# Cross attention, Mamba block and cross attention in one program: the same instructions in another order on five engines

## The chip, the core and the metric

The kernel runs on one core of a Trainium2 chip. The core has a matrix engine (PE), a vector engine (DVE), an activation engine (ACT), a general engine (POOL) and an engine that here only issues DMAs (SP). Each takes its own instructions strictly in order; between engines only semaphores order the work. The metric is the time of one execution on the device in microseconds (us), lower is better.

## What is computed

Input are 64 sequences of 128 tokens with 256 features (`x`) and as many of context (`ctx_1024`). Everything is computed for each sequence by itself, in float32.

```python
# layer 0: attention to the context, 16 heads of 16, masked queries, then layer norm
q, k, v = relu(x @ Wq + bq), relu(ctx @ Wk + bk), relu(ctx @ Wv + bv)
scores = where(mask_of_query, q k^T / sqrt(16), 1e-9)
x = layernorm(softmax(scores) @ v + x) * gamma + beta
# layer 1a: a Mamba block, 8 heads of 64, state of 128
zxbcdt = rms(x, norm_w) @ in_proj_w                       # z | xBC | dt
xBC = silu(conv_b + causal convolution of xBC over 4 taps)
dt = softplus(dt + dt_bias); decay = exp(dt * -exp(A_log))
h_t = h_(t-1) * decay_t + (dt_t * xh_t) outer B_t;  y_t = h_t C_t + D_skip * xh_t
x = x + rms(y * silu(z), gnorm_w) @ out_proj_w
# layer 1b: layer norm, then attention to the context, 8 heads of 32
x = x + softmax(LN(x) Wq (ctx Wk)^T / sqrt(32) + padding) @ (ctx Wv) @ Wo
```

## The kernel before

**Groups and halves.** Two sequences are a group; there are 32 groups (`NG`) of two halves (`NB`). All 32 go through one software pipeline that is written out by hand. A small function is a unit of work on one engine: `tap(g, 7)` is one of the 18 convolution steps of group g, `scan(g, 1)` the scan of its second half. It waits for its semaphores, issues one or a few instructions and raises a semaphore. Each engine has a list of unit calls, and a loop over `s` (called a round here) runs the list once a round: `q(s - 2, 0)` works on group s - 2, `wp(s - 7, 0)` on the group that began five rounds earlier. The offsets need only agree within an engine, since nothing but semaphores ties the engines together. In the steady part each engine does the work of one group in a round, from six neighbouring groups.

**Order and banks.** The list sets the order of an engine. The table `USES` gives for each use of a PSUM bank (`("k1", 0, 4), 1` is: unit k1, part 0, four rounds behind, in bank 1) the order of the uses, and `bank()` works out from it which semaphore tells that the user before in the bank is done; PE waits for it.

**Units that are spoken of here,** with their lines. PE: `q`, `k`, `cp`, `z` are groups of six matmuls of L301; `v` L333 and L336; `sA` L355 and `sT` L386 and L391 are the scores of layer 0; `tn` L366; `av` L411; `ot`, `nt`, `bx`, `ht`, `tC` are transposes at L397; `bd` L456 transposes the decays; `gm` L486; `y` L508; `o` L522 and L523; `q1`, `k1` L535; `v1` L573; `sC` L593 and L597 are the scores of layer 1b; `oC` L622; `wp` L635 is the last projection. DVE: `dk` L847 copies the decays out of PSUM to `decT`; `scan` L883 builds the matrix `L` of decay products from `DB`; `lg` L892 multiplies it; `tap` L859, `xc` L872 convolution; `rc` L739, `xo` L749, `bs` L758, `bg` L764, `xs` L770, `x2` L780 are the end of layer 0; `mA` L718 and `mC` L968 row maxima; `k2` L706; `r1`, `hh` L928, `hs` L935, `hg`, `hm` the second norm; `nm` L730 and L732; `yd` L911; `sz` L900. POOL: `xr` L1457 adds `xt`, the token-major x, to the attention's output in `xa`; `rs` L1464 and L1466; `qm` L1449; `dx` L1484; `xd` L1493; `ga` L1502; `s2_` L1508 and L1510; `nC` L1532. ACT: `split_x` L1127 among others.

**The way of the decays.** `dk` writes decT; SP writes it to HBM (`dec_out`, L266), waits until it has landed, and reads it back broadcast to 128 partitions, 512 KB for each half (`dec_in`, L274), into `DB`. The scan of the half waits for that. `y` on PE needs the scan, and `bd` of the next group stands behind `y` on PE.

**SP** has nine units a round, all in one queue. A unit that waits holds all behind it.

```python
def load_t(g):
    if ok(g):
        if g > 0:
            e.wait_ge(s_xr, 2 * g)
        e.dma_start(xt[:, :, :], a["xt"][g]).then_inc(d_xt, 16)
```

There is one buffer each for xT, cT, cU and xt, so that a load waits until the group before has been read.

Of the kernel before, what the change touches and what calls it, by code (L numbers as in the profile page):

```python
# [12 lines left out]
NG = 32  # L13
# [20 lines left out]
]  # L34
STEPS = NG + 7


def program(nc, a):
    with ExitStack() as ctx:
# [171 lines left out]
        def sync(e):  # L211
# [84 lines left out]
        def tensor(e):  # L296
# [345 lines left out]
            for s in range(STEPS):  # L642
                gm(s - 5, 0)
                z(s - 5, 1)
                ht(s - 6, 1)
                av(s - 4, 6)
                bx(s - 5, 1)
                y(s - 5, 0)
                q1(s - 6, 0)
                av(s - 4, 7)  # L650
                q1(s - 6, 1)
                gm(s - 5, 1)
                ot(s - 4, 1)
                sC(s - 6, 0)
                k1(s - 4, 0)
                v(s - 3, 0)
                o(s - 5, 0)
                sA(s - 3, 0)
                wp(s - 7, 0)
                k1(s - 4, 1)  # L660
                y(s - 5, 1)
                nt(s - 4, 0)
                sA(s - 3, 1)
                tC(s - 6, 0)
                q(s - 2, 0)
                tC(s - 6, 1)
                dp(s - 4, 0)
                cp(s - 4, 0)
                q(s - 2, 1)
                cp(s - 4, 1)  # L670
                tC(s - 6, 2)
                tn(s - 3, 0)
                o(s - 5, 1)
                cp(s - 4, 2)
                tC(s - 6, 3)
                cp(s - 4, 3)
                oC(s - 6, 0)
                oC(s - 6, 1)
                v1(s - 4, 0)
                k(s - 2, 0)  # L680
                sT(s - 3, 0)
                bd(s - 4, 0)
                k(s - 2, 1)
                cp(s - 4, 4)
                av(s - 3, 0)
                ht(s - 5, 0)
                cp(s - 4, 5)
                tn(s - 3, 1)
                av(s - 3, 1)
                av(s - 3, 2)  # L690
                av(s - 3, 3)
                sT(s - 3, 1)
                ot(s - 3, 0)
                z(s - 4, 0)
                bx(s - 4, 0)
                av(s - 3, 4)
                av(s - 3, 5)

        def vector(e):
# [325 lines left out]
            for s in range(STEPS):  # L1025
                tap(s - 4, 1)
                tap(s - 4, 2)
                dc(s - 4, 0)
                dc(s - 4, 1)
                tap(s - 4, 3)  # L1030
                dc(s - 4, 2)
                r1(s - 5, 1)
                hm(s - 5, 0)
                xc(s - 4, 0)
                tap(s - 4, 4)
                dc(s - 4, 3)
                hh(s - 5, 1)
                dc(s - 4, 4)
                dc(s - 4, 5)
                tap(s - 4, 5)  # L1040
                dc(s - 4, 6)
                dc(s - 4, 7)
                dc(s - 4, 8)
                dc(s - 4, 9)
                dc(s - 4, 10)
                xc(s - 4, 1)
                hs(s - 5, 1)
                dc(s - 4, 11)
# [10 lines left out]
                xc(s - 4, 2)
                tap(s - 4, 12)  # L1060
                hm(s - 5, 1)
                tap(s - 4, 13)
                xc(s - 4, 3)
                tap(s - 4, 14)
                tap(s - 4, 15)
                tap(s - 4, 16)
                tap(s - 4, 17)
                k2(s - 2, 1)
                xc(s - 4, 4)
                xc(s - 4, 5)  # L1070
                rc(s - 3, 0)
                xo(s - 3, 0)
                scan(s - 4, 0)
                bs(s - 3, 0)
                bg(s - 3, 0)
                lg(s - 4, 0)
                xs(s - 3, 0)
                sz(s - 4, 0)
                sz(s - 4, 1)
                yd(s - 4, 0)  # L1080
                x2(s - 3, 0)
                scan(s - 4, 1)
                lg(s - 4, 1)
                mC(s - 5, 0)
                rc(s - 3, 1)
                xo(s - 3, 1)
                mC(s - 5, 1)
                kk1(s - 3, 0)
                bs(s - 3, 1)
                bg(s - 3, 1)  # L1090
                mC(s - 5, 2)
                mC(s - 5, 3)
                r1(s - 4, 0)
                rC(s - 5, 0)
                xs(s - 3, 1)
                x2(s - 3, 1)
                mA(s - 2, 0)
                mA(s - 2, 1)
                hh(s - 4, 0)
                mA(s - 2, 2)  # L1100
                mA(s - 2, 3)
                rC(s - 5, 1)
                fin(s - 6, 0)
                kk1(s - 3, 1)
                nm(s - 2, 0)
                yd(s - 4, 1)
                rC(s - 5, 2)
                nl(s - 3, 0)
                nl(s - 3, 1)
                mA(s - 2, 4)  # L1110
                mA(s - 2, 5)
                mA(s - 2, 6)
                mA(s - 2, 7)
                hs(s - 4, 0)
                rC(s - 5, 3)
                d0(s - 3, 0)
                d0(s - 3, 1)
                tap(s - 3, 0)
                hg(s - 4, 0)

        def scalar(e):
# [244 lines left out]
            for s in range(STEPS):  # L1366
                eA(s - 4, 0)
                eA(s - 4, 1)
                eA(s - 4, 2)
                ac(s - 5, 4)  # L1370
                he(s - 6, 0)
                th(s - 5, 3)
                eA(s - 4, 3)
                nt_(s - 4, 1)
                ac(s - 5, 5)
                ke(s - 3, 1)
                oa(s - 4, 0)
                th(s - 5, 4)
                th(s - 5, 5)
                hx(s - 6, 1)  # L1380
                eA(s - 4, 4)
                eA(s - 4, 5)
                xhe(s - 5, 0)
                eA(s - 4, 6)
                zt(s - 5, 0)
                eA(s - 4, 7)
                zt(s - 5, 1)
                split_x(s - 2)
                he(s - 6, 1)
# [264 lines left out]
```

## Time and profile before

| | us |
|---|---|
| median of 3 runs | 1593.8 (1592.28 to 1598.35) |
| the profiled execution | 1593.56 |
| its span, first to last instruction | 1591.5 |
| PE busy | 1433.3 (90% of the span) |
| DVE busy | 1317.2 (83%) |
| ACT busy | 1030.6 (65%) |
| POOL busy | 881.3 (55%) |
| mean granted clock of PE | 0.977 of full speed |
| DMA | 86.99 MB, 55 GB/s on the mean |

An engine's busy time is the sum of its instructions with overlap taken out; a matmul's end is modelled. "issue" as a releaser means that the profile shows no event that the engine waited for. Busy shares alone don't tell what sets the time: the rows below do, by stretch, by wait, by the chain and by single instructions.

### The profile page before, as it was taken

How to read it: one execution, taken by the hardware profiler on the slowest of the kernel's cores; microseconds unless marked ns; L12 is line 12 of the kernel's file. 1: busy time of each engine (PE TensorE's matmuls, PEld its weight loads, DVE VectorE, ACT ScalarE, POOL GpSimd, SP SyncE). 2: the span in 40 equal slices, each digit the busy share in tenths (PEclk: the TensorE clock that was granted, in tenths of full speed). 3: DMA queues.
4: the chain of work that ended last, by engine and by line, in shares of the span. 5: the costliest groups of instructions: out<-in, count | busy, mean ns of one | idle time of the engine just before them, and what ended most of it. 6: DMA issues, size and time to landing. Idle time of an engine off the chain costs nothing.

```text
span 1591.5 us, 43440 instructions
## 1 busy us (share of the span) xinstructions
PE 1433.3 (90%) x15912; PEld 1185.8 (75%) x15912; DVE 1317.2 (83%) x3115; ACT 1030.6 (65%) x3044; POOL 881.3 (55%) x1125
## 2 busy tenths in 40 slices
PE   1889999999999999989988888999999999999976
PEld 1677787877777877777877777877778787778764
DVE  5688888888888888878888888889888888888882
ACT  1546767766667766666766666766666766676664
POOL 6354564565555556544556554556555566556553
PEclk9998999999999999999999999999999999999998
DMA  4111122112122101212201212201212211211110
GB/s 140 42 57 57 49 65 65 42 35 64 56 63 64 62 16 63 65 55 65 65 25 51 64 55 64 64 14 64 65 55 65 65 34 42 64 55 49 48 34 20
DMA packets 41136, 86.99 MB, mean 55 GB/s; under 512 B 5728, under 2 KB 10976, under 8 KB 40928
## 3 DMA queue, kind: packets, MB, share of 16 engines
q1 hardware_dynamic: 40928, 84.23, 17.4%
q8 instruction: 129, 2.11, 0.6%
q14 instruction: 79, 0.65, 0.1%
HBM read 75.53 MB, written 8.68 MB: 53 GB/s over the span
## 4 chain that ended last, share of the span: by engine, by line
PE 43%; DVE 18%; POOL 13%; DMA 13%; ACT 6%; issue 4%; SPq 3%; DVEq 0%; POOLq 0%; ACTq 0%
DMA DB<-dec_scratch 12%; PE bank L301 11%; DVE L L883 5%; PE bank L397 5%; POOL DX L1484 4%; ACT PC L1339 4%; PE bank L522 4%; PE bank L635 4%; PE bank L573 4%; DVE L L892 3%; POOL Y L1502 2%; PE bank L508 2%; PE bank L386 2%; PE bank L355 2%; PE bank L622 2%
## 5 line engine op out<-in xcount | busy, mean ns | idle before, releaser
L859 DVE SCALAR_TENSOR_TENSOR ACC<-bank,cw,ACC 128x250 f32<-128x250 f32 (+2 forms) x576 | 271.5, 472 | 20.5 <-ACT ACC L1266 9.8
L883 DVE TENSOR_TENSOR_SCAN L<-DB,id 128x1024 f32<-128x1024 f32 x64 | 184.0, 2876 | 62.7 <-DMA DB<-dec_scratch 62.7
L1339 ACT ACTIVATE PC<-bank,stc 128x128 f32<-128x128 f32 x512 | 180.7, 377 | 77.6 <-DVE stc L968 76.8
L301 PE MATMUL bank<-xnT,wnl 128*128 128x256 f32 x640 | 199.2, 311 | 1.9 <-ACT PTA L1178 0.5
L301 PE MATMUL bank<-xnT,wnh 128*128 128x256 f32 x640 | 179.3, 280 | 0.0
L301 PE MATMUL bank<-xnL,wnh 128*128 128x256 f32 x640 | 179.1, 280 | 0.0
L1484 POOL TENSOR_TENSOR DX<-XC,pc 128x512 f32<-128x512 f32 x64 | 126.2, 1972 | 73.7 <-DVE XC L872 73.7
L718 DVE TENSOR_REDUCE sta<-bank 128x4 f32<-128x512 f32 x256 | 160.9, 680 | 2.8 <-PE bank L355 2.8
L1178 ACT ACTIVATE PTA<-bank 128x512 f32<-128x512 f32 x256 | 141.7, 595 | 8.6 <-PE bank L391 8.6
L1532 POOL TENSOR_TENSOR PC<-PC,stc 128x512 f32<-128x512 f32 x128 | 133.3, 1042 | 10.3 <-DVE stc L975 10.3
L1502 POOL TENSOR_TENSOR Y<-Y,SZ 128x512 f32<-128x512 f32 x64 | 88.8, 1388 | 90.1 <-DVE Y L911 90.1
L522 PE MATMUL bank<-wout,Y 128*128 128x256 f32 x512 | 124.4, 387 | 6.2 <-POOL SQ L1510 6.2
L301 PEld LDWEIGHTS bank<-xnT,wnl 128*128 128x128 f32 x640 | 121.3, 189 | 10.9 <-DVE KT L706 8.5
L1266 ACT ACTIVATE ACC<-bank,cw 128x256 f32<-128x256 f32 x192 | 107.7, 561 | 32.0 <-PE bank L301 27.9
L1524 POOL TENSOR_SCALAR stb<-stb 128x1 f32<-128x1 f32 x64 | 14.0, 219 | 204.8 <-DVE stb L941 204.8
L508 PE MATMUL bank<-L,XH 128*64 128x128 f32 x1024 | 72.9, 286 | 58.8 <-issue 53.5
L301 PEld LDWEIGHTS bank<-xnL,wnh 128*128 128x128 f32 x640 | 121.3, 190 | 0.0
L301 PEld LDWEIGHTS bank<-xnT,wnh 128*128 128x128 f32 x640 | 120.6, 188 | 0.0
L508 PEld LDWEIGHTS bank<-L,XH 128*64 128x64 f32 x1024 | 57.7, 140 | 76.3 <-issue 73.9
L1283 ACT ACTIVATE XH<-bank 128x512 f32<-128x512 f32 x64 | 38.3, 598 | 114.3 <-PE bank L508 89.7
L1339 ACT ACTIVATION_READ_ACCUMULATOR PC<-bank,stc 128x1 f32 x512 | 110.8, 216 | 0.0
L522 PEld LDWEIGHTS bank<-wout,Y 128*128 128x128 f32 x512 | 93.8, 193 | 17.9 <-DVE L L892 3.9
(185 smaller groups left out, 4343.9 us busy)
## 6 DMA issues: line engine op xcount, KB each, us to landing
DB<-dec_scratch SPq DMA_DIRECT2D x64, 512.0 KB, 7.6
xT<-in_xT SPq DMA_DIRECT2D x32, 256.0 KB, 2.7
cT<-in_cT SPq DMA_DIRECT2D x32, 256.0 KB, 2.8
cU<-in_cT SPq DMA_DIRECT2D x32, 256.0 KB, 2.9
xt<-in_xt SPq DMA_DIRECT2D x32, 256.0 KB, 5.0
out_x<-X SPq DMA_DIRECT2D x32, 256.0 KB, 8.1
QM<-qm_rows SPq DMA_DIRECT2D x32, 128.0 KB, 3.1
XC<-in_win SPq DMA_DIRECT2D x2, 644.0 KB, 5.2
```

The source lines that it names most:

```text
L301: mm = e.matmul(t[:, c0:c0 + T], wt[:, k, m:m + 128], x[:, k, :], start=(n == 0), stop=(n == 5))
L508: mm = e.matmul(t[64 * (h % 2):64 * (h % 2) + 64, (h // 2) * 128:(h // 2 + 1) * 128], XH[:, h * 64:h * 64 + 64], L[:, h, :], start=True, s ...
L522: e.matmul(t[:, 0:256], Y[b][:, kk * 128:(kk + 1) * 128], wout[:, kk, :], start=(kk == 0), stop=(kk == 3))
L718: e.tensor_reduce(sta[ns % 4][:, 4 * j:4 * j + 4], t[:, :].rearrange("p (i k) -> p i k", i=4), AX_X, ALU.max, negate=True).then_inc(s_mA, 1)
L859: e.scalar_tensor_tensor(out=w, in0=t[:, 0:T].rearrange("p (b t) -> p b t", b=NB)[:, :, 0:125 + k], scalar=cw[:, c, k:k + 1], in1=w, op0=A ...
L883: e.tensor_tensor_scan(L[:, :, :].rearrange("p h t -> p (h t)"), DB[b][:, :], id8[:, :, :].rearrange("p h t -> p (h t)"), 0.0, ALU.mult, A ...
L1178: e.activation(PTA[n % 4][:, :, :], t[:, :].rearrange("p (i k) -> p i k", i=4), ACT.Exp).then_inc(s_eA, 1)
L1266: e.activation(ACC[n % 3][:, :, :], t[:, 0:T].rearrange("p (b t) -> p b t", b=NB), ACT.Identity, bias=cw[:, c, 4:5], scale=cw[:, c, 3:4]). ...
L1339: op = e.activation(PC[n % 5][:, p, :], t[:, p * 128:(p + 1) * 128], ACT.Exp, bias=stc[g % 4][:, 4 * i + p:4 * i + p + 1], accum_out=stc[g ...
L1484: e.tensor_tensor(cv(DX[:, :]), XC[g % 2][:, 0:4, b * 128:(b + 1) * 128], pc[:, 14:18].unsqueeze(2).to_broadcast([128, 4, 128]), ALU.mult) ...
L1502: e.tensor_tensor(cv(Y[b][:, :]), cv(Y[b][:, :]), SZ[:, :, b * 128:(b + 1) * 128], ALU.mult).then_inc(s_ga, 1)
L1532: e.tensor_tensor(PC[n % 5][:, :, :], PC[n % 5][:, :, :], stc[g % 4][:, 16 + 4 * i:20 + 4 * i].unsqueeze(2).to_broadcast([128, 4, 128]), A ...
```

## The change

No instruction is added, taken away or altered. The lists of all five engines are permuted, with them the table USES (other banks, other order), and the offsets of the units in their rounds. STEPS goes from NG + 7 to NG + 11 since SP's offsets are larger by a constant. The DVE, ACT, PE and POOL lists have 100, 66, 55 and 26 unit calls as before. The diff, cut to SP and to the places that matter here:

```diff
 USES = [
-    (("gm", 0, 5), 5), (("z", 1, 5), 3), (("ht", 1, 6), 6), (("bx", 1, 5), 0), (("y", 0, 5), 7), (("q1", 0, 6), 6),
...
+    (("wp", 0, 5), 6), (("bx", 1, 3), 1), (("k1", 0, 2), 5), (("sA", 4, 1), 7), (("sA", 5, 1), 2), (("sA", 6, 1), 3),
...
-STEPS = NG + 7
+STEPS = NG + 11
...
             for s in range(STEPS):
-                dec_in(s - 4, 1)
-                store(s - 7)
-                load_x(s)
-                load_m(s)
-                dec_out(s - 3)
-                load_c(s)
-                load_u(s - 2)
-                load_t(s - 2)
-                dec_in(s - 3, 0)
+                load_x(s - 5)
+                load_c(s - 5)
+                load_t(s - 7)
+                dec_out(s - 7)
+                load_m(s - 5)
+                load_u(s - 6)
+                dec_in(s - 7, 0)
+                store(s - 11)
+                dec_in(s - 7, 1)
```

**SP.** Before, one round from the store of the decays (L266) to the next loads of xT and QM:

```order
L266 DMA dec_scratch<-decT 16x128
L241 DMA cT<-in_cT 128x512
L254 DMA cU<-in_cT 128x512
L247 DMA xt<-in_xt 128x512
L274 DMA DB<-dec_scratch 128x1024 x2
L280 DMA out_x<-X 128x512
L235 DMA xT<-in_xT 128x512
L260 DMA QM<-qm_rows 128x256
```

and now, from the same store to the load of xt that stands ahead of the next store:

```order
L266 DMA dec_scratch<-decT 16x128
L260 DMA QM<-qm_rows 128x256
L254 DMA cU<-in_cT 128x512
L274 DMA DB<-dec_scratch 128x1024
L280 DMA out_x<-X 128x512
L274 DMA DB<-dec_scratch 128x1024
L235 DMA xT<-in_xT 128x512
L241 DMA cT<-in_cT 128x512
L247 DMA xt<-in_xt 128x512
```

cT and xt went from ahead of the two DB loads to behind them, xT came in behind them too, QM went ahead of them, and the store of the output stands between them. The xt in the last row is that of the group after the one whose decays are stored, as it was before.

**DVE, ahead of the scan of the first half** (L883; L739 and L749 make xa, L758 and L764 are its mean and variance, L718 and L892 stand further on). Before:

```order
L706 TENSOR_SCALAR KT<-bank,kb 128x2x128
L872 SCALAR_TENSOR_TENSOR XC<-bank,ACC 128x256 x2
L739 RECIPROCAL sta<-bank 128x16
L749 TENSOR_TENSOR xa<-bank,sta 128x256
L883 SCALAR_TENSOR_TENSOR L<-DB,id 128x1024
L758 BN_STATS sta<-xa 128x6
L764 BN_AGGR sta<-sta 128x2
L892 TENSOR_TENSOR L<-L,bank 128x1024
L770 SCALAR_TENSOR_TENSOR xa<-xa,sta,gam 128x256
L900 SCALAR_TENSOR_TENSOR SZ<-SZ,bank 128x512 x2
L911 TENSOR_TENSOR Y<-bank,DX 128x512
```

and now:

```order
L739 RECIPROCAL sta<-bank 128x16
L749 TENSOR_TENSOR xa<-bank,sta 128x256
L859 SCALAR_TENSOR_TENSOR ACC<-bank,cw,ACC 128x2x125
L859 SCALAR_TENSOR_TENSOR ACC<-bank,cw,ACC 128x2x126
L859 SCALAR_TENSOR_TENSOR ACC<-bank,cw,ACC 128x2x127
L758 BN_STATS sta<-xa 128x6
L764 BN_AGGR sta<-sta 128x2
L706 TENSOR_SCALAR KT<-bank,kb 128x2x128
L872 SCALAR_TENSOR_TENSOR XC<-bank,ACC 128x256
L770 SCALAR_TENSOR_TENSOR xa<-xa,sta,gam 128x256
L872 SCALAR_TENSOR_TENSOR XC<-bank,ACC 128x256
L883 SCALAR_TENSOR_TENSOR L<-DB,id 128x1024
```

L758, which needs POOL's sum of xa and xt, went from behind the scan to ahead of it, with the aggregate and L770. L706 (the second half's k) stands behind L758 now.

**PE, around y of the first half** (L508; L397 with xh is ht, with OA ot; L593 and L597 are sC). Before, y stood ahead of q1 and sC:

```order
L397 MATMUL bank<-ident,xh 128x128 x2
L411 MATMUL bank<-PTA,V 32x128 x4
L397 MATMUL bank<-ident,XC 128x128 x4
L508 MATMUL bank<-L,XH 64x128 x8
L535 MATMUL bank<-HT,wq 128x256 x2
L411 MATMUL bank<-PTA,V 32x128 x4
L535 MATMUL bank<-HT,wq 128x256 x2
L486 MATMUL bank<-XC 128x128
L397 MATMUL bank<-ident,OA 128x128 x4
L593 MATMUL bank<-K1T,Q1T 128x128 x16
L597 MATMUL bank<-maskb,onesb 128x512 x4
```

and now sC comes first, then z, and y behind it (the last rows are the first of z):

```order
L355 MATMUL bank<-KT,QT 128x256 x8
L411 MATMUL bank<-PTA,V 32x128 x8
L535 MATMUL bank<-HT,wq 128x256 x2
L397 MATMUL bank<-ident,OA 128x128 x4
L535 MATMUL bank<-HT,wq 128x256 x2
L486 MATMUL bank<-XC 128x128
L397 MATMUL bank<-ident,XC 128x128 x4
L593 MATMUL bank<-K1T,Q1T 128x128 x16
L597 MATMUL bank<-maskb,onesb 128x512 x4
L301 MATMUL bank<-xnT,wnl 128x256
L301 MATMUL bank<-xnL,wnh 128x256
L301 MATMUL bank<-xnT,wnh 128x256
```

On PE L456 (bd) is followed by y after 13 us of work before; now nearly half a round's work stands between them.

## Rows read from the trace of the kernel before

**Rows 1.** By stretch: length, then PE, PEld, DVE, ACT, POOL busy (count), clock, DMA
```profile
34.70:197.60 162.90, 145.86 (x1603) 119.52 (x1603) 130.49 (x302) 95.36 (x259) 80.82 (x101) 0.96 0.18 54
197.60:1474.80 1277.20, 1194.13 (x13420) 991.12 (x13420) 1095.76 (x2593) 865.26 (x2565) 724.39 (x918) 0.98 0.18 54
1474.80:1591.50 116.70, 93.32 (x890) 75.15 (x890) 74.29 (x186) 67.22 (x218) 56.24 (x68) 0.93 0.11 35
...
622.37:668.31 45.94, 43.52 (x498) 36.33 (x498) 40.69 (x99) 32.13 (x96) 28.24 (x34) 1.00 0.19 56
```

**Rows 2.** Waits from 197.6 to 1474.8 us: who for whom, total, times, longest
```profile
DVE L L883 <- DMA DB<-dec_scratch: 55.9, 27, 3.5
...
PE bank L508 <- issue: 48.0, 23, 3.2
...
PE bank L635 <- ACT V L1160: 23.1, 19, 1.9
```

**Rows 3.** The chain in order of time, one step: start, length, what
```profile
642.08 0.22 PE bank L456
...
642.39 0.29 DVE decT L847
...
644.53 6.33 DMA DB<-dec_scratch
...
650.95 2.29 DVE L L883
```

**Rows 4.** SP's queue in the next step: start, length of the issue, line
```profile
688.65 0.32 SPq L266 DMA_DIRECT2D dec_scratch<-decT  x1
...
691.38 0.42 SPq L280 DMA_DIRECT2D out_x<-X  x1
```

**Rows 5.** Issue to landing, us: window 640:660, then 686:702, then xt and out_x overall
```profile
cT<-in_cT SPq DMA_DIRECT2D x1, 256.0 KB, 2.8
cU<-in_cT SPq DMA_DIRECT2D x1, 256.0 KB, 3.0
...
out_x<-X SPq DMA_DIRECT2D x1, 256.0 KB, 7.4
...
out_x<-X SPq DMA_DIRECT2D x1, 256.0 KB, 8.9
...
DMA to landing us min/median/max: 3.0/5.0/7.0
...
DMA to landing us min/median/max: 2.0/8.1/10.1
```

**Rows 6.** PE's timeline over one step: start, length, line, idle before
```profile
642.01 0.28 PE L456 MATMUL bank<-ident,dts 128*16 128x128 f32 x1
...
654.99 1.09 PE L508 MATMUL bank<-L,XH 128*64 128x128 f32 x16 [0.89 <-DVE L L892]
...
659.44 1.17 PE L593 MATMUL bank<-K1T,Q1T 32*128 32x128 f32 x32 [0.22 <-issue]
...
660.76 1.13 PE L535 MATMUL bank<-cU,wk 128*128 128x256 f32 x4
...
687.96 0.28 PE L456 MATMUL bank<-ident,dts 128*16 128x128 f32 x1
```

**Rows 7.** DVE's timeline: four maxima, the scan with its wait, x2
```profile
674.36 2.47 DVE L718 TENSOR_REDUCE sta<-bank 128x4 f32<-128x512 f32 x4
...
698.41 2.29 DVE L883 TENSOR_TENSOR_SCAN L<-DB,id 128x1024 f32<-128x1024 f32 x1 [2.74 <-DMA DB<-dec_scratch]
...
704.89 0.47 DVE L780 SCALAR_TENSOR_TENSOR X<-xa,sta,bet 128x256 f32<-128x256 f32 x1
```

**Rows 8.** POOL's L1457; all scans (ns min/median/max); DX beside a scan
```profile
696.44 0.73 POOL L1457 TENSOR_TENSOR xa<-xa,xt 128x256 f32<-128x256 f32 x1 [3.37 <-DMA xt<-in_xt]
...
L883 DVE TENSOR_TENSOR_SCAN L<-DB,id x64: 2276/2988/3366, 87.8 to 1544.6; 128x1024 f32<-128x1024 f32 x64
...
658.62 2.98 POOL DX L1484
```

More of the change, by code:

```diff
@@ new lines, in tensor @@
+                y(s - 3, 1)
+                cp(s - 2, 1)
+                tC(s - 4, 2)
+                tn(s - 1, 0)
+                tC(s - 4, 3)
+                oC(s - 4, 0)
+                z(s - 2, 0)
+                oC(s - 4, 1)
+                v1(s - 2, 0)
+                sT(s - 1, 0)
+                o(s - 3, 1)
+                cp(s - 2, 2)
+                q(s, 0)
+                bd(s - 2, 0)
+                q(s, 1)
+                cp(s - 2, 3)
+                av(s - 1, 0)
+                cp(s - 2, 4)
@@ new lines, in tensor @@
+                ht(s - 3, 0)
+                av(s - 1, 1)
+                av(s - 1, 2)
+                av(s - 1, 3)
+                k(s, 0)
+                tn(s - 1, 1)
+                cp(s - 2, 5)
+                ot(s - 1, 0)
+                k(s, 1)
+                sT(s - 1, 1)
+                v(s, 0)
+                ht(s - 3, 1)
+                av(s - 1, 4)
+                av(s - 1, 5)
+                sA(s, 0)
+                av(s - 1, 6)
+                av(s - 1, 7)
+                q1(s - 3, 0)
@@ L1059, in vector @@
[L1059 to L1075, printed above, removed]
@@ new lines, in vector @@
+                tap(s - 3, 5)
+                dk(s - 3, 0)
+                hh(s - 4, 1)
+                tap(s - 3, 6)
+                tap(s - 3, 7)
+                hs(s - 4, 1)
+                xc(s - 3, 1)
+                tap(s - 3, 8)
+                tap(s - 3, 9)
+                tap(s - 3, 10)
+                hg(s - 4, 1)
+                tap(s - 3, 11)
+                xc(s - 3, 2)
+                tap(s - 3, 12)
+                xc(s - 3, 3)
+                tap(s - 3, 13)
+                k2(s - 1, 0)
@@ new lines, in vector @@
+                tap(s - 3, 14)
+                hm(s - 4, 1)
+                rc(s - 2, 0)
+                xo(s - 2, 0)
+                tap(s - 3, 15)
+                tap(s - 3, 16)
+                tap(s - 3, 17)
+                bs(s - 2, 0)
+                bg(s - 2, 0)
+                k2(s - 1, 1)
+                xc(s - 3, 4)
+                xs(s - 2, 0)
+                xc(s - 3, 5)
+                scan(s - 3, 0)
+                x2(s - 2, 0)
+                mA(s - 1, 0)
+                mA(s - 1, 1)
@@ new lines, in vector @@
+                mA(s - 1, 2)
+                rc(s - 2, 1)
+                xo(s - 2, 1)
+                mA(s - 1, 3)
+                lg(s - 3, 0)
+                bs(s - 2, 1)
+                mC(s - 4, 0)
+                bg(s - 2, 1)
+                xs(s - 2, 1)
+                mC(s - 4, 1)
+                mC(s - 4, 2)
+                rC(s - 4, 0)
+                yd(s - 3, 0)
+                sz(s - 3, 1)
+                mC(s - 4, 3)
+                rC(s - 4, 1)
+                x2(s - 2, 1)
@@ new lines, in vector @@
+                fin(s - 5, 0)
+                kk1(s - 2, 0)
+                nm(s - 1, 0)
+                mA(s - 1, 4)
+                rC(s - 4, 2)
+                mA(s - 1, 5)
+                scan(s - 3, 1)
+                nl(s - 2, 0)
+                nl(s - 2, 1)
+                lg(s - 3, 1)
+                mA(s - 1, 6)
+                d0(s - 2, 0)
+                d0(s - 2, 1)
+                mA(s - 1, 7)
+                rC(s - 4, 3)
+                kk1(s - 2, 1)
+                yd(s - 3, 1)
@@ new lines, in vector @@
+                r1(s - 3, 0)
+                tap(s - 2, 0)
+                tap(s - 2, 1)
+                tap(s - 2, 2)
+                dc(s - 2, 0)
+                dc(s - 2, 1)
+                dc(s - 2, 2)
+                hh(s - 3, 0)
+                xc(s - 2, 0)
+                dc(s - 2, 3)
+                nm(s - 1, 1)
+                dc(s - 2, 4)
+                sz(s - 2, 0)
+                dc(s - 2, 5)
+                dc(s - 2, 6)
+                dc(s - 2, 7)
+                hs(s - 3, 0)
@@ L1121, in scalar @@
+                dc(s - 2, 8)
+                dc(s - 2, 9)
         def scalar(e):
@@ new lines, in scalar @@
+                nt_(s - 2, 1)
+                ac(s - 3, 5)
+                ke(s - 1, 1)
+                th(s - 3, 4)
+                hx(s - 4, 1)
+                eA(s - 2, 4)
+                eA(s - 2, 5)
+                th(s - 3, 5)
+                eA(s - 2, 6)
+                eA(s - 2, 7)
+                he(s - 4, 1)
+                oa(s - 2, 1)
+                ve(s - 1, 0)
+                q1e(s - 4, 0)
+                q1e(s - 4, 1)
+                n1(s - 2, 0)
+                split_x(s)
@@ new lines, in scalar @@
+                xhe(s - 3, 0)
+                eC(s - 4, 0)
+                zt(s - 3, 1)
+                eC(s - 4, 1)
+                eC(s - 4, 2)
+                n1(s - 2, 1)
+                nx(s - 2, 0)
+                qq(s - 3, 0)
+                xhe(s - 3, 1)
+                nx(s - 2, 1)
+                pC(s - 4, 0)
+                pC(s - 4, 1)
+                nh(s - 2, 0)
+                nh(s - 2, 1)
+                eC(s - 4, 3)
+                ac(s - 2, 0)
+                split_c(s)
@@ new lines, in scalar @@
+                nt_(s - 1, 0)
+                pC(s - 4, 2)
+                de(s - 2, 0)
+                de(s - 2, 1)
+                de(s - 2, 2)
+                qq(s - 3, 1)
+                pC(s - 4, 3)
+                th(s - 2, 0)
+                dq(s - 2, 0)
+                zt(s - 2, 0)
+                ac(s - 2, 1)
+                oT(s - 4, 0)
+                v1e(s - 2, 0)
+                dd(s - 2, 0)
+                eA(s - 1, 0)
+                eA(s - 1, 1)
+                da(s - 2, 0)
```

287 lines of the change are left out of this document (65 added, 222 removed), and 20 rows, old and new, of the table USES.

## Prediction

> **What bounds the kernel now.** I read the busy time by stretches first [rows 1]. Between the first output projection of group 0 (197.6 us) and that of group 27 (1474.8 us) lie 27 equal steps: 1277.2 us, so 47.3 us a step. PE is busy for 1194.1 us of them and idle for 83.1 us, which is 3.1 us a step. In a step at full clock PE is busy 43.5 us: that is the floor of a step. Ahead of the stretch PE idles 17 us (after its first 34.7 us), behind it 23 us.
>
> The waits come second [rows 2]. Of the 83 us, 48 are spent ahead of L508 (unit y), 23 ahead of L635 (unit wp). DVE at the same time waits 55.9 us in 27 pieces ahead of L883, the scan, for the DMA that brings DB. The reader is to see that these are one chain, told in order of time by the chain of waits [rows 3]: PE's transpose L456 (unit bd) ends at 642.30, DVE copies decT until 642.68, SP issues dec_scratch, the DB load is issued at 644.53 and lands 6.3 us later, and the scan starts at 650.95. From there it takes 4.0 us to L508 at 654.99 [rows 6] and 33.0 us of PE work and two small waits to the next L456. So the step's loop is: 0.7 us (L456 to the end of the copy) + 9.4 (copy to landing of DB: 1.85 to its issue and 7.6 at the median of the page; 8.2 here) + 4.1 + 33.2 = 47.4 us, which is the 47.3 that the steps take. The bound is this loop, not PE's work.
>
> **What the change does to that loop.** Nothing is added or removed: 43.5 us of PE work and DVE's some 41 us a step stay. Three things move. That STEPS is 43 and no longer 39 costs nothing: the offsets of SP are larger by as much, and PE has work in 37 rounds on either side (q at s - 2 to wp at s - 7 before, q at s to wp at s - 5 now).
>
> First, the DB load goes out behind two transfers (QM, cU: 384 KB) and no longer behind three (768 KB), and DVE has more work between the copy L847 and the scan. In the kernel before DVE ran dry 7.1 us after the copy (it ended at 688.62, the scan's wait began at 698.41 - 2.74 = 695.67 [rows 7]). Now hh, hs, three more taps, one more xc and k2 stand there too (2.8 us), and L758 with its aggregate and xs (0.9), and nm is gone (0.3): 10.5 us up to the scan. DB should land 7 to 9 us after the copy. So its wait, 55.9 us in the 27 steps, goes to about nothing.
>
> Second, PE has y of the first half late in the round and bd at its middle. From L508 to the next L456 stand all units but those from L456 to L508. These are eight groups of six L301 at 0.72 us, v 2.1, sT 1.5, sA 1.07, eight av 2.8, two ht 0.6, two ot 1.3, two q1 1.9, gm and bx 0.8, sC 1.3, tn 0.1: 19.2 to 19.8 us, taken as 19.5, by the distances of starts in PE's timeline from the first to the second L456 [rows 6]. That leaves 43.5 - 19.5 = 24.0 us in place of 33.0.
>
> Third, and this is the term that decides, **the load of xt is now the last of SP's burst**. SP issues in order and everything behind dec_scratch waits for the copy of decT. Before, the burst was cT, cU, xt, DB, DB, out_x. Now it is QM, cU, DB, out_x, DB, xT, cT, xt. The xt that comes in with it is the one that POOL adds in the same half round (L1457), and DVE's bn_stats L758 of the first half needs that sum. L758 stood behind the scan; now it stands in front of it. So the added wait is DVE's at L758, and queued behind it are k2 of the second half, xs, the scan, four of the row maxima L718 and lg; behind L1457 on POOL are QT's second product, the root for x2 and DX. PE's ht of the second half needs the bank that k2 frees, and sC the banks that the maxima free.
>
> When does xt land? The trace has no xt at that place, so I bound it. The last transfer of the burst before is out_x: issued 2.75 us after the copy ended (691.38 against 688.62) [rows 4], it lands 7.4 us and 8.9 us after its issue in two bursts and 8.1 at the median [rows 5]: 10.2, 11.7 and 10.9 us after the copy, for 2048 KB. The new burst has 2432 KB. cT and cU, issued 0.52 us apart, land 0.7 us apart, so 384 KB more cost 1.05 us at best, and at the burst's mean pace (10.9 us for 2048 KB) 2.0. I take 1.05, since they are plain rows like cT and cU: xt lands 11.9 us after the copy (11.2 to 13.6). Below that stands only the case that xt keeps the landing time that it has now, 5.0 us (3.0 to 7.0) [rows 5], behind an issue at 4.2 us after the copy: 9.2 us. Its present time is that of the third in line, hence I take the last's.
>
> The Trainium skill, "DMA: Bandwidth & Descriptors" (Queues, rings and completion order), says that each DMA engine consumes descriptors in ring order, and that a semaphore increment lands only after all earlier writes of that engine. By that rule xt, last in the queue, is last to be complete; the order of the landings above agrees.
>
> **The sum.** L456 to the copy's end 0.7; xt's landing 11.9; L1457 0.73 and two handoffs, 0.85 [rows 8]; L758, its aggregate, k2, xc, xs, xc 2.0; scan 2.2, x2 0.4, four L718 at 0.6 and rc with xo 0.8 [rows 7], 5.9 with a handoff; then PE's sC 1.3 (659.44 to 660.76 [rows 6]) and two groups of z 1.5, 2.8; y to L456 24.0. Together **48.1 us** against 47.3. 27 steps give +22 us, three steps of the fill that hold the same loop +2. The profiled execution was 1593.56 us (2.1 above its span, and the median of the runs is 1593.8): 1593.6 + 24 = **1618 us**. Fill and drain otherwise stay as they are, with 40 us of idle time between them.
>
> One price is uncertain within this. POOL and DVE hold each other up: the scan takes 2.28 us or up to 3.37, and DX on POOL 2.98 instead of 1.05 [rows 8]. In the new order the two adds L1508 and L1510, which o of the first half needs, come beside the second scan. If the scan gets in between, o starts up to 1.0 us late; if the order of arrival is kind, nothing. DX beside the first scan costs 0.4 likewise. I take none of it and keep 0 to 1.4 us a step for the range. The Trainium skill, "SBUF — State Buffer" (SBUF: two separate sides), calls this an exclusive lock between GpSimd and a VectorE instruction with two SBUF inputs, held for the whole instruction: by it the whole 1.0 falls due wherever the two meet.
>
> **Rivals.** (1) *xt keeps its 5.0 us*, landing 9.2 us after the copy, or the burst's slow middle falls away. DVE reaches L758 8.5 us after the copy anyway (the 7.1 from above, + 2.8 for what is new ahead of it, - 1.4 for nm and for one k2 and two xc that now stand behind). The loop is 48.1 - 2.7 = 45.4, to 45.8 with DX beside the scan: 1593.6 - 30 x 1.7 = 1543 us (1530 to 1570), faster. It decides at a landing 11.1 us after the copy: below that the new loop is shorter than 47.3. For it: out_x had landed at 10.2 in one of the bursts; against it: 384 KB more are ahead. (2) *xt lands before DVE wants it*, within 8.5 us. Then the loop goes along DVE: 0.7 + 10.5 + 5.9 + 2.8 + 24.0 = 43.9, and with DX beside the scan 44.3: 1593.6 - 30 x 3.0 = 1504 us (1490 to 1530). This would need 2432 KB in 8 us, 0.3 MB each us; the burst before made 2048 KB in 10 to 11.7. The same skill page on DMA (Anatomy of one DMA) fits 2.0 us + bytes / 436 GB/s: an estimate by it is 7.7 us for the burst and this rival's time; here the burst before took 9.8 to 11.3 us from its first issue where that fit gives 6.8, so the trace speaks against it. (3) *A wash*: xt between 10.2 and 11.1, a loop of 46.4 to 47.3, 1570 to 1600 us. (4) *Both go wrong*: xt late at 13 us and POOL's adds behind the scan, a loop of 50 us: 1593.6 + 30 x 2.7 = 1675 us.
>
> **Chances.** The forecast 0.54 (1602 to 1650), rival 1 0.20, rival 2 0.07, rival 3 0.12, rival 4 0.07. A difference under 0.5% (8 us) is about what a measurement of this kernel can't tell from none. Faster: rivals 1 and 2 and a third of 3, 0.31; same 0.09; slower 0.60. The range leaves out rival 2, the fast edge of rival 1 and rival 4: 1540 to 1650. The forecast's own range is 1602 to 1650.
>
> **What the profile after would show.** Steps of about 48 us. DVE's wait ahead of L883 for DB gone; in its place one ahead of L758, some 3 to 4 us a step, for POOL's L1457, which waits for the DMA of xt. xt's landing near 7.7 us after its issue, not 5.0. PE idle 4 to 5 us a step, ahead of L397 (ht), of L593 (sC) and maybe of L522 (o). The chain of waits goes through the xt load. Wrong would be: xt's landing near 5 us, steps of 45 us; or a wait at a place that I have priced at nothing, ACT's split of xT (its load lands some 10 us after the copy and is wanted near 14), or PE's bank waits between L635 and L456.

## The result and the profile after

The changed kernel takes 1686.5 us (median of 4 runs, 1684.09 to 1697.73) against 1594.35 us for the kernel before: 1.0583 times as long, with a 95% interval of 1.0536 to 1.0629. It is slower, as forecast, but by 92 us and not by 24, and outside the range of 1540 to 1650 us. The profiled execution is the longest of the four, 1697.7 us; its span is 1695.4 us.

By stretch, with the columns of [rows 1] and the same cuts (ahead of the first L635, its steps 1 to 27, what is behind), and one single step:

```profile
35.30:205.20 169.90, 144.38 (x1583) 119.97 (x1581) 124.78 (x296) 88.91 (x239) 71.44 (x95) 0.91 0.17 51
205.20:1553.50 1348.30, 1227.89 (x13422) 1018.74 (x13420) 1079.36 (x2593) 849.24 (x2565) 716.53 (x919) 0.95 0.15 51
1553.50:1695.40 141.90, 108.88 (x912) 87.51 (x910) 81.49 (x193) 71.25 (x238) 63.17 (x75) 0.81 0.09 31
830.42:881.27 50.85, 46.13 (x499) 38.15 (x499) 39.95 (x96) 31.46 (x96) 26.52 (x35) 0.93 0.16 51
```

The 27 steps take 1348.3 us, 49.94 each; they took 47.30. So 71 of the span's 103.9 us more are in the steps, 25.2 in the drain (141.9 against 116.7) and 7.6 ahead of the first L635. DVE is busy no longer than before (1079 against 1096 us); PE is 34 us busier with as many instructions, at a clock of 0.95 instead of 0.98.

Who waits for whom from 300 to 1500 us (24 steps: total, times, longest), in the place of [rows 2]:

```profile
POOL xa L1457 <- DMA xt<-in_xt: 129.5, 24, 7.2
...
DVE sta L758 <- POOL xa L1457: 86.5, 24, 5.0
...
PE bank L397 <- DVE KT L706: 79.5, 24, 4.6
...
PE bank L355 <- DVE X L981: 14.2, 24, 0.7
...
PE bank L445 <- DVE xnL L794: 12.7, 24, 0.5
```

DVE's waits ahead of L883 are gone, and so are PE's ahead of L508 and L635. In their place stands one chain: the DMA of xt, POOL's sum, DVE's mean L758 (3.6 us a step), k2 behind it, and PE's ht (L397, 3.3 us a step). The last two rows are small (0.6 and 0.5 us a step), and they are the ones that the forecast did not have.

The chain of waits over one step (start, length, what), in the place of [rows 3]. It starts at PE's L456 and ends at the next:

```profile
830.42 0.12 PE bank L456
...
834.97 7.33 DMA xt<-in_xt
...
842.37 0.73 POOL xa L1457
...
843.12 0.44 DVE sta L758
...
844.19 0.69 PE bank L397 x2
...
852.83 1.17 PE bank L593 x32
...
854.33 0.69 DVE stc L968
...
859.93 0.61 DVE X L981
...
860.67 1.18 PE bank L355 x16
...
863.30 2.04 DVE L L883
...
865.95 0.14 DVE xnL L794
...
866.82 1.03 PE bank L445 x8
...
881.27 0.12 PE bank L456
```

SP's queue in this step, the first load of the burst and its last two, and the landings over the whole run (compare [rows 4, 5]):

```profile
831.32 0.41 SPq L260 DMA_DIRECT2D QM<-qm_rows  x1
...
834.27 0.66 SPq L241 DMA_DIRECT2D cT<-in_cT  x1
834.97 1.20 SPq L247 DMA_DIRECT2D xt<-in_xt  x1
```
```profile
DMA to landing us min/median/max: 4.7/6.8/8.0
```

xt is issued 4.05 us after the end of the copy (830.92) and lands 11.4 us after it, and 10.6 in the step behind; over the bursts of the 27 steps that is 8.7 to 12.6 us, 11.4 at the median. Its landing takes 6.8 us from the issue at the median, where it took 5.0.

### The profile page after: what moved, and what is told of

The parts are those of the page before. It is cut to its first block, busy times and chain, and to the rows that moved or that the text cites. A ratio compares the mean times of both kernels' runs of the same rounds, so it can differ in the third digit from the quotient of the medians.

```text
span 1695.4 us, 43439 instructions
## 1 busy us (share of the span) xinstructions
PE 1481.7 (87%) x15912; PEld 1226.8 (72%) x15912; DVE 1302.8 (77%) x3115; ACT 1012.1 (60%) x3044; POOL 871.5 (51%) x1125
## 4 chain that ended last, share of the span: by engine, by line
PE 48%; DVE 21%; DMA 16%; issue 5%; SPq 5%; POOL 4%; ACT 1%; DVEq 0%; POOLq 0%; ACTq 0%
DMA xt<-in_xt 13%; PE bank L301 10%; PE bank L355 5%; PE bank L522 4%; PE bank L535 4%; PE bank L397 4%; DVE L L883 4%; PE bank L573 4%; DVE stc L968 3%; PE bank L411 3%; DMA dec_scratch<-decT 3%; PE bank L508 2%; PE bank L593 2%; PE bank L386 2%; PE bank L622 2%
## 5 line engine op out<-in xcount | busy, mean ns | idle before, releaser
L1457 POOL TENSOR_TENSOR xa<-xa,xt 128x256 f32<-128x256 f32 x64 | 46.5, 726 | 347.4 <-DVE xa L749 180.3
L718 DVE TENSOR_REDUCE sta<-bank 128x4 f32<-128x512 f32 x256 | 168.1, 678 | 27.7 <-PE bank L355 27.6
L883 DVE TENSOR_TENSOR_SCAN L<-DB,id 128x1024 f32<-128x1024 f32 x64 | 177.1, 2767 | 0.0
L1532 POOL TENSOR_TENSOR PC<-PC,stc 128x512 f32<-128x512 f32 x128 | 138.7, 1084 | 65.2 <-DVE stc L975 65.2
L355 PE MATMUL bank<-KT,QT 32*128 32x256 f32 x1024 | 101.0, 522 | 23.8 <-DVE X L981 16.5
L1339 ACT ACTIVATION_READ_ACCUMULATOR PC<-bank,stc 128x1 f32 x512 | 120.7, 236 | 0.0
L397 PE MATMUL bank<-ident,xh 128*128 128x128 f32 x128 | 31.6, 335 | 100.6 <-DVE KT L706 91.8
L1449 POOL TENSOR_TENSOR QT<-QT,QM 128x256 f32<-128x256 f32 x64 | 48.1, 752 | 136.8 <-DMA QM<-qm_rows 128.4
L758 DVE BATCH_NORM_STATS2 sta<-xa 128x6 f32<-128x256 f32 x64 | 27.1, 424 | 109.5 <-POOL xa L1457 109.5
L1187 ACT ACTIVATE OA<-bank 128x512 f32<-128x512 f32 x64 | 38.3, 599 | 118.8 <-PE bank L411 118.8
```

The lines of the kernel that those rows point to most:

```text
L355: mm = e.matmul(ts[j][:, m * 256:(m + 1) * 256], QT[g % 2][r, m, b * 128:(b + 1) * 128], KT[g % 2][r, m, b, :, :], start=True, stop=True)
L397: mm = e.transpose(t[:, c0 + i * 128:c0 + (i + 1) * 128], src(i), ident[:, :])
L718: e.tensor_reduce(sta[ns % 4][:, 4 * j:4 * j + 4], t[:, :].rearrange("p (i k) -> p i k", i=4), AX_X, ALU.max, negate=True).then_inc(s_mA, 1)
L883: e.tensor_tensor_scan(L[:, :, :].rearrange("p h t -> p (h t)"), DB[b][:, :], id8[:, :, :].rearrange("p h t -> p (h t)"), 0.0, ALU.mult, A ...
L1339: op = e.activation(PC[n % 5][:, p, :], t[:, p * 128:(p + 1) * 128], ACT.Exp, bias=stc[g % 4][:, 4 * i + p:4 * i + p + 1], accum_out=stc[g ...
L1532: e.tensor_tensor(PC[n % 5][:, :, :], PC[n % 5][:, :, :], stc[g % 4][:, 16 + 4 * i:20 + 4 * i].unsqueeze(2).to_broadcast([128, 4, 128]), A ...
```

## The experiments

All runs stand in one table; "step" is the mean distance of the 27 starts of L635, "drain" the span from the 28th to the end, both from the profiled execution. Each ratio is against runs of the kernel before that were made beside it, with medians of 1594.35 to 1601.4 us.

| run | median us | against before, 95% interval | first L635 | step | drain |
|---|---|---|---|---|---|
| before | 1594.35 | 1 | 197.6 | 47.30 | 116.7 |
| after | 1686.51 | 1.0583 (1.0536 to 1.0629) | 205.2 | 49.94 | 141.9 |
| xt_first | 1573.13 | 0.9856 (0.9771 to 0.9942) | 192.1 | 46.16 | 132.9 |
| xt_fourth | 1567.48 | 0.9819 (0.9746 to 0.9893) | 195.1 | 45.78 | 131.7 |
| bs_behind | 1655.47 | 1.0356 (1.0277 to 1.0435) | 201.7 | 48.44 | 134.9 |
| pe_filled | 1680.66 | 1.0517 (1.0440 to 1.0594) | 206.5 | 49.42 | 138.5 |
| before_xt_last | 1597.08 | 0.9991 (0.9963 to 1.0020) | 191.4 | 47.48 | 119.2 |
| bs_behind_qm | 1594.50 | 0.9985 (0.9963 to 1.0007) | 196.2 | 46.71 | 132.9 |
| qm_last | 1558.33 | 0.9744 (0.9712 to 0.9777) | 192.8 | 45.72 | 129.9 |
| qm_last_fin | 1532.86 | 0.9589 (0.9561 to 0.9617) | 190.5 | 44.77 | 129.4 |
| after_fin | 1658.09 | 1.0363 (1.0292 to 1.0433) | 204.0 | 48.72 | 140.0 |
| before_db_first | 1531.63 | 0.9590 (0.9542 to 0.9638) | 187.1 | 45.34 | 118.4 |

### Is it the place of the xt load? (xt_first, xt_fourth)

```diff
 # xt_first, SP's list of the kernel after
-                load_t(s - 7)
                 dec_out(s - 7)
+                load_t(s - 6)
                 load_m(s - 5)
 # xt_fourth
-                load_t(s - 7)
...
                 dec_in(s - 7, 0)
+                load_t(s - 6)
                 store(s - 11)
```

> The changed kernel, but SP issues the load of xt right behind the store of the decays (first of the burst, not ninth); nothing else moves. Theory A (the late xt, through L758 ahead of the scan, holds the loop, and PE's idle time that comes of it also costs granted clock): xt lands about 3 us after its issue, the wait of L758 goes, DB still lands before DVE's 10.5 us of work are done, the clock stays up; the loop is 0.7 + 10.5 + 5.9 + 28.4 less the slow clock = 45 us a step and the whole about 1550 us (1530 to 1575). Theory B (the new order of PE and its banks is what costs: the waits of L355 for L981 and of L445 for L794, and xt's wait is only where the slack shows): the wait moves to another place and the step stays at 49 to 50 us, 1660 to 1690 us.

> The changed kernel with the load of xt issued behind the first DB load, fifth in the burst, ahead of the store of the output. Theory A with transfers that land in the order of issue: xt lands where the output's store lands now, 7 to 8.3 us after the copy of decT, so L758 waits 0 to 0.8 us; 45 to 46 us a step, 1550 to 1585 us, at most 20 us above the kernel with xt first. Were the landing not by place in the queue but by what xt is, it would keep its 6.8 us: 9 us after the copy, a step of 46 to 47 us, 1590 us. Theory B: 1660 to 1690 us.

One line moved in SP's list takes 113 to 119 us off, more than the 92 us that the change cost, and leaves the new order a little faster than the old (1.4 and 1.8%; the intervals end at 0.994 and 0.989). So the whole loss hangs on the one load; even the steps' slower clock goes with it (1.00 in the window of xt_fourth's steps, 0.95 after). xt_first is inside its range of 1530 to 1575 us, but 23 us above the 1550 that it was expected at. Its chain of waits shows what holds it next:

```profile
814.52 0.29 DVE decT L847
...
815.66 4.07 DMA QM<-qm_rows
...
819.80 0.73 POOL QT L1449
...
820.80 0.57 POOL stb L1526
821.39 0.16 DVE stb L948
```

With xt first, QM is the next late load: POOL waits for it, and the root L1526 that DVE's hm (L948) wants is queued behind. This is a part of the 23 us and not all: qm_last below, with QM's load at the end of the burst for a later group, is 15 us under xt_first. Landing follows the place in the burst: xt lands 2.8 us after its issue at the median as the second, 5.2 as the fifth behind dec_scratch, QM, cU and DB, 6.8 as the last. The Trainium skill, "DMA: Bandwidth & Descriptors" (Queues, rings and completion order), has each DMA engine take descriptors in ring order; the trace agrees: all 240 transfers that SP issues in the steps of the kernel after land in the order of issue.

### By how many ways does a late xt hold the loop? (bs_behind, bs_behind_qm, before_xt_last)

```diff
 # bs_behind, DVE's list
-                bs(s - 2, 0)
-                bg(s - 2, 0)
                 k2(s - 1, 1)
                 xc(s - 3, 4)
-                xs(s - 2, 0)
                 xc(s - 3, 5)
                 scan(s - 3, 0)
-                x2(s - 2, 0)
+                bs(s - 2, 0)
+                bg(s - 2, 0)
+                xs(s - 2, 0)
                 mA(s - 1, 0)
                 mA(s - 1, 1)
+                x2(s - 2, 0)
 # bs_behind_qm: that, and in POOL's list
+                qm(s - 1, 1)
                 xr(s - 2, 0)
-                qm(s - 1, 1)
```

> The changed kernel with SP's order as it is (xt last), but on DVE L758, L764 and L770 of the first half stand behind the scan, as before the change, and L706 of the second half, L872 and the scan no longer wait for xt; x2 stands behind two of the maxima. Theory A: the scan starts 10 us after the copy and ends at 12.5, xt lands at 11.0 and POOL's sum is done at 11.8, so nobody waits for it; PE's L397 with xh is not held, the clock stays up. 44.5 to 46 us a step, 1540 to 1580 us. If instead xt's late landing holds the loop by itself (through POOL's queue: L1449, dx and xd stand behind the sum), still 48 us a step, 1630 us. Theory B: 1660 to 1690 us.

It missed the 1540 to 1580 us: 1655 us, which is 31 of the 119 us that an early xt gives. What fits is the expectation's other case, a step of 48 us because the late xt holds the loop through POOL's queue: the step is 48.44. PE's waits of bs_behind, from 300 to 1400 us:

```profile
PE bank L355 <- POOL QT L1449: 62.1, 22, 3.3
```

That is 2.8 us each time. POOL has QT's second product (L1449) behind its sum L1457 with xt, and the scores L355 want QT. The prediction listed that product among what is queued behind L1457, and gave it no price.

> The kernel after with two edits: on DVE the mean and variance of the first half (L758, L764) and what hangs on them stand behind k2 and the scan, as in the run bs_behind, and on POOL the second product of QT (qm, L1449) stands ahead of the sum with xt (xr, L1457) and no longer behind it. xt is still the last load of SP's burst. Theory (late xt holds the loop by exactly two ways, DVE's L758 ahead of the scan, and QT's product behind L1457 for the scores L355): both are gone, PE's wait ahead of L355 for POOL's L1449 (62 us in bs_behind) goes to below 10 us, the step goes from 48.5 to about 46 us and the time to 1560 to 1590 us, near the runs with an early xt (1567, 1573). Rival (a third way, say DX or the roots on POOL behind L1457, or PE's slow clock): 1620 us or more.

The second way is closed (the wait is not in the list any more), and the step falls by another 1.7 us. Of the expected 46 it keeps 0.7 us more, and the median is 4.5 us above the expected 1560 to 1590. POOL's timeline, then DVE's, of bs_behind_qm show the third way:

```profile
838.09 2.36 POOL L1457 TENSOR_TENSOR xa<-xa,xt 128x256 f32<-128x256 f32 x1 [3.54 <-DMA xt<-in_xt]
```
```profile
837.65 2.28 DVE L883 TENSOR_TENSOR_SCAN L<-DB,id 128x1024 f32<-128x1024 f32 x1
840.48 0.43 DVE L758 BATCH_NORM_STATS2 sta<-xa 128x6 f32<-128x256 f32 x1 [0.56 <-POOL xa L1457]
```

xt lands while the scan runs, and POOL's sum, 0.72 us elsewhere, ends 0.5 us after the scan does: it takes 2.36 us. DVE then waits for it, 0.6 us a step (14.2 us in 23 waits from 300 to 1400 us), and PE's wait ahead of sC for the maxima L718 behind it is 26.4 us there, against 7.7 in xt_fourth. The step is 0.9 us longer than that of xt_fourth. That this wait is the cause is read from the traces: no run took it away. The Trainium skill, "SBUF — State Buffer" (SBUF: two separate sides), calls the port pair that DVE and POOL share a lock held for the whole instruction; the trace agrees in kind, since the sum ends only behind the scan.

```diff
 # before_xt_last, SP's list of the kernel before
+                load_t(s - 3)
                 load_x(s)
...
                 load_u(s - 2)
-                load_t(s - 2)
```

> The kernel before with one unit of SP moved: the load of xt goes from behind cU to behind the store of the output, last of SP's burst, where it stands in the kernel after. In this order of DVE the mean L758 stands behind the scan. Theory (a late xt costs only where DVE's first-half mean stands ahead of the scan and the row maxima): xt lands about 2 to 3 us later than before, 8 to 11 us after the copy of the decays, while L758 is due some 12 us after the copy; the loop keeps its 47.3 us step and the time is within 1.5% of the kernel before, 1575 to 1610 us, perhaps a few us less since DB is issued with less ahead of it. Rival (a load at the end of the burst costs in any order, through POOL's queue or otherwise): a step of about 50 us as in the kernel after, 1660 to 1690 us.

It held: 0.9991, a step of 47.48 us, with xt landing 7.7 us after its issue at the median. In the order of before, the same late load costs nothing on balance. DVE's waits of before_xt_last, from 300 to 1400 us, show the trade. In the same stretch of the kernel before, L883 waits 50.8 us for DB and L758 5.2 us for POOL's sum; now it is

```profile
DVE sta L758 <- POOL xa L1457: 36.3, 40, 2.4
...
DVE L L883 <- DMA DB<-dec_scratch: 21.7, 18, 3.0
```

### What does the slow clock cost? (pe_filled)

Near the end of the 3.5 us in which PE waits for k2 its granted clock falls. Windows of the kernel after within the step shown above (length, PE's busy time, and so on; the clock is the third number from the end):

```profile
840.50:843.50 3.00, 0.20 (x2) 0.00 (x0) 0.38 (x1) 0.56 (x2) 1.13 (x2) 1.00 0.11 41
...
844.50:850.50 6.00, 6.00 (x54) 3.79 (x53) 5.58 (x7) 1.47 (x3) 1.26 (x2) 0.50 0.01 3
850.50:853.50 3.00, 2.89 (x38) 2.50 (x39) 2.16 (x4) 1.87 (x6) 0.73 (x1) 1.00 0.01 3
```

In this step 6 us of PE work run at 0.50 of full speed, 1.2 GHz, right behind the wait, and DVE waits 1.2 us for one of them, the transpose L397 ahead of L739. Over the steps that wait is smaller: 12.8 us in 15 of 22 steps from 300 to 1400 us. The run adds work to PE ahead of the wait:

```diff
 # in v of PE, before its own matmuls into the same bank
+                    for n in range(28):
+                        e.matmul(t[:, 0:T], wqh[:, 0, 0:128], wkh[:, 0, :], start=True, stop=True)
```

> The changed kernel with 28 more matmuls of 256 columns on constants at the start of each unit v; their result is overwritten by v's own. They take 3.3 us of PE just ahead of the place where PE idles 3.5 to 4.6 us for L706, so they should cost no time themselves. Theory of the clock: after the idle time the granted clock stands at 0.50 for some 6 us and the matmuls of L355, L411 and L535 there take twice as long, worth 1.3 to 2 us a step; with the idle time filled the clock stays at 1.0, and the kernel is faster by 27 x 1.3 to 2: 1635 to 1655 us in spite of 896 more matmuls. Rival (the slow stretch is no cost, since DVE is the one that is waited for there): 1680 to 1700 us.

The rival held. The clock in the steps' window is 1.00, PE has 1.7 us more to do in a step (1272.55 us in 1334.50), and the step is 49.42 us: only 0.5 us shorter, about what DVE's wait ahead of L739 was, which is gone (0.2 us in all are left from 300 to 1400 us). The chain of waits of pe_filled, whose lines stand two lower, shows why: it runs on DVE alone from L760 (L758) to L983 (L981).

```profile
831.50 7.37 DMA xt<-in_xt
...
839.71 0.44 DVE sta L760
...
855.09 0.61 DVE X L983
...
855.84 1.18 PE bank L357 x16
```

From POOL's sum to PE's scores DVE has 16 us of its own work, with no wait above 0.1 us in between. Whatever PE does in that time, the scores come 16 us after L758.

### The unpriced end of DVE's row (after_fin, qm_last, qm_last_fin)

```diff
 # after_fin, and qm_last_fin with SP's list below: DVE
+                fin(s - 5, 0)
                 x2(s - 2, 1)
-                fin(s - 5, 0)
 # qm_last and qm_last_fin: SP
-                load_t(s - 7)
+                load_m(s - 5)
                 dec_out(s - 7)
-                load_m(s - 5)
                 load_u(s - 6)
                 dec_in(s - 7, 0)
+                load_t(s - 6)
                 store(s - 11)
```

> The kernel after with one edit on DVE: L981 (fin) stands ahead of the second half's L780 (x2) and no longer behind it. SP's burst is that of the kernel after, with xt last and late. Theory (of the 1.8 us by which its step was longer than forecast, about half is the path from L758 along DVE to L981 and PE's L355, which the forecast had put on sC and PE alone): the step falls by 0.7 to 1.0 us from 49.94, the time to 1655 to 1665 us, and PE's wait ahead of L355 for L981 (0.7 us a step) goes. Rival (the late xt hides it, or the next wait takes its place): within 6 us of the kernel after, 1680 to 1690.

> The kernel after with SP's order changed: behind the store of the decays stand cU, DB of the first half, xt, the store of the output, DB of the second half, xT, cT, and QM last, where QM belongs to the group one round further on (it has two buffers), so that it is wanted a whole round later. In the run xt_fourth QM went first and xt fourth. Theory: with xt in time nothing of SP's burst holds the loop any more, POOL's 100 us of waits for QM go to nothing and the time gains little over xt_fourth: 1555 to 1570 us, a step of 45.5 us, set by DVE's row of work from the scan to L981. Rival (QM's place mattered for the loop through hm and the scan): 1545 or less.

> As qm_last, and on DVE L981 (fin, the last sum of the output, whose bank PE's scores L355 of the same group need) stands ahead of L780 of the second half (x2) and no longer behind it. Theory (the loop with xt in time goes along DVE to L981 and from there to PE's L355, which idles 0.6 us a step for it): the wait ahead of L355 goes, 0.4 to 0.6 us a step, against qm_last 12 to 18 us less, about 1545 us. Rival (the next wait, L445 for L794, 0.5 us a step, takes its place, since DVE has the same work up to there): the same time as qm_last within 5 us.

after_fin and qm_last came where they were expected, though after_fin's step fell by 1.2 us and not by 0.7 to 1.0. qm_last_fin kept its mechanism and missed its size: 25 us off qm_last and not 12 to 18. L981 one place earlier takes 28 us off the kernel after (1.2 us a step) and 25 us off qm_last (0.95 us a step). PE's waits of qm_last, then those of qm_last_fin, both from 300 to 1400 us:

```profile
PE bank L397 <- DVE sta L718: 14.3, 24, 0.8
PE bank L355 <- DVE X L981: 14.1, 24, 0.6
PE bank L445 <- DVE xnL L794: 12.6, 24, 0.5
```
```profile
PE bank L397 <- DVE sta L718: 14.0, 24, 0.8
...
PE bank L445 <- DVE xnL L794: 4.4, 23, 0.2
```

The swap frees L355 (0.6 us a step) and most of L445's wait as well, since L445 stands at the end of the same row. What moved behind, x2 of the second half, makes neither PE nor DVE wait. qm_last against xt_fourth gives 9 us and not more: with xt in time, QM's place matters little, though POOL's waits for QM, 100.1 us in bs_behind_qm from 300 to 1400 us, are gone.

### Was the loop of the kernel before what the prediction said? (before_db_first)

```diff
 # SP's list of the kernel before
                 dec_out(s - 3)
+                dec_in(s - 3, 0)
                 load_c(s)
                 load_u(s - 2)
                 load_t(s - 2)
-                dec_in(s - 3, 0)
```

> The kernel before with one unit of SP moved: the load of DB of the first half stands directly behind the store of the decays, ahead of cT, cU and xt (768 KB) instead of behind them. Theory (the loop of the kernel before is held by the landing of DB at 9.4 us after the copy of the decays; DVE runs dry 7.1 us after it): DB lands 5 to 6 us after the copy, DVE's 56 us of waits ahead of L883 go, the scan starts about 2 us earlier, a step of 45.2 to 45.8 us and a time of 1535 to 1560 us. Rival (with DB early another piece is as late: cT or xt behind 512 KB more, or PE's V wait): 1580 us or more.

It held: 1531.6 us, 4.1% faster than before, with one unit of SP moved; DVE waits no longer for DB, and 2.0 us a step are gone. The loop over DB was the bound. It is as fast as the best version of the new order (1532.9): its step is 0.6 us longer, its drain 11 us shorter.

## Why the prediction was wrong

**Right.** The bound of before (47.4 us over DB) was right, by before_db_first. So was the term that decides: xt last in the burst, DVE waiting ahead of L758 and not ahead of L883, 3 to 4 us a step (3.6), PE ahead of L397 (3.3). The size of the landing was close: 11.9 us after the copy forecast, 11.4 measured at the median; it was 7.7 us from the issue by the forecast and is 6.8 at the median. The bound from out_x's place [rows 5] was a sound one. Rival 4, 1675 us, has nearly the measured time but not its cause: xt did not land at 13 us, and POOL's adds L1508 and L1510 were not held up (0.75 us at most).

**Wrong: the sum behind the landing.** Term by term, in the step shown above:

| term | forecast | measured |
|---|---|---|
| L456 to the copy's end | 0.7 | 0.5 |
| xt's landing | 11.9 | 11.4 |
| L1457 and handoffs | 0.85 | 0.8 |
| L758 to the scan (845.11) | 2.0 | 2.0 |
| scan to sC (852.83) | 5.9 | 7.7 |
| sC and z to y (855.77) | 2.8 | 2.9 |
| y to L456 | 24.0 | 25.5 |
| sum | 48.1 | 50.85 (mean of 27: 49.94) |

Two terms were too small. The timelines of DVE, POOL and PE have the 1.8 us of the first. The scan takes 2.8 us beside DX where the sum had 2.2: a price that I had listed and set to nothing, and it falls due in every step (the 54 scans of the 27 steps, two each, take 2.79 to 2.83 us). No run moved DX away from the scan, so this size is read and not tried. And L739 waits 1.16 us for PE's transpose of OA, which runs late at half clock.

```profile
844.70 1.06 POOL L1484 TENSOR_TENSOR DX<-XC,pc 128x512 f32<-128x512 f32 x1
```
```profile
845.11 2.80 DVE L883 TENSOR_TENSOR_SCAN L<-DB,id 128x1024 f32<-128x1024 f32 x1
...
851.24 0.26 DVE L739 RECIPROCAL sta<-bank 128x16 f32<-128x16 f32 x1 [1.16 <-PE bank L397]
```
```profile
844.19 0.69 PE L397 MATMUL bank<-ident,xh 128*128 128x128 f32 x2 [3.49 <-DVE KT L706]
844.81 1.08 PE L411 MATMUL bank<-PTA,V 128*32 128x128 f32 x16
845.82 2.09 PE L355 MATMUL bank<-KT,QT 32*128 32x256 f32 x16
```

L355 takes 2.09 us here and 1.18 at 860.67. The second term, "y to L456 24.0 us", was a sum of PE's work alone: it assumed that after y PE has no wait up to L456. That step failed. PE waits there for L981 (0.6 us a step) and L794 (0.5), since DVE comes to both only at the end of the 16 us that start at L758; the other 0.4 us of this term is PE work that takes longer than I had summed. The loop runs from L758 down DVE's row to L981; for sC and its mask DVE waits only 0.24 us on that way in this step (at L968). I named "PE's bank waits between L635 and L456" as something that would prove me wrong, and then didn't walk DVE's row down to them; the pieces were in the profile of before, where DVE is busy 40.7 of 45.9 us of a step [rows 1]. after_fin shows the size: 1.2 of the 1.84 us by which the mean step missed. On the mean of the steps between 300 and 1500 us, L758 to L981 takes 16.2 us in the kernel after, 14.9 in after_fin and 15.3 in pe_filled.

The clock, which the prediction didn't treat, is the smaller part: pe_filled gave 0.5 us a step with it undisturbed, though it also paid for 28 matmuls. The 0.5 and the 1.2 come from separate runs, and were not added up in one.

**Wrong: "fill and drain otherwise stay".** The 28th L635 to the end takes 25.2 us longer, the time to the first 7.6. The fill's part is the late xt: with xt early the first L635 is at 190.5 to 195.1 us (205.2 after), and at 196.2 in bs_behind_qm, where xt is late but less stands behind it. Of the drain's, 11 to 12 us are the late xt (141.9 after against 129.9 in qm_last, 140.0 in after_fin against 129.4 in qm_last_fin), and some 13 us the new order's own; in the order of before it is 116.7 to 119.2. PE's clock in it is 0.81 after, 0.89 in qm_last and was 0.93. PE's busy time in the drain is 108.9, 98.6 and 93.3 us with about as many matmuls (912, 914, 890), so that most of the late xt's 12 us goes with the slower clock, and more than half of the new order's own 13 is idle time. Why the new order drains slower wasn't tried and stays open. In sum: steps 27 x 1.84 = 50, fill 6, drain 25, together 81, is what the profiled execution lies above the forecast (1697.7 - 1618 = 80). The other three runs are 11 to 14 us shorter than the profiled one.

**The chance.** The rivals all varied xt's landing. A case in which xt lands as forecast and the row behind it is longer was missing, so the range ended at 1650.

## What to carry to other kernels

Order the loads that stand behind one wait in a single queue by when their readers want them, not by what they are for: one load of 256 KB moved from the end of the burst to its middle was worth 119 us here, and one of 512 KB moved to its head 64 us in the kernel before. When a late event holds an engine, walk that engine's whole row from there to each place where another engine waits for it; a path counted on the other engine's work alone is a lower bound. Moving one reader behind the wait is not enough if another engine has the same late event in front of other work in its queue.

## What the runs showed of the hardware

- Near the end of the burst of nine SP's issue itself grows: L241 and L247 take 0.66 and 1.20 us in the step shown, 0.98 and 0.52 in the next and 0.69 and 0.50 at the median, against 0.43 for L260 at its head. In before_xt_last, where the burst has seven, L247 as the last takes 0.42. The last issue comes 3.65 us after the burst's first load (831.32).
- The burst of 2432 KB takes 11.0 us from that first issue (831.32) to the last landing (842.30), which is also the median of the 27 steps (8.3 to 12.2). The Trainium skill, "DMA: Bandwidth & Descriptors" (Anatomy of one DMA), fits 2.0 us + bytes / 436 GB/s for a single DMA that GpSimd issues; for this burst from SP's queue that is 7.7 us by estimate, and the trace is 3.3 us above it.
- PE's granted clock stays at 1.00 through most of an idle stretch of 3.5 us and is 0.50 in the 6 us of full work behind it, then 1.00 again; in the next step it is 0.50 for 3.4 us. The price falls on the work behind the wait, not on the wait.
